# One-hot rows of a graph kernel's bucket pass: a single VectorE compare in place of GpSimd and ScalarE, and a transpose moved to the end of TensorE's step

## The reference

```python
# layers 1 and 2
z = concat([x[dst], x[src], attr]); m = sigmoid(z @ Wf + bf) * softplus(z @ Ws + bs)
h = leaky_relu(graph_norm(segment_sum(m, dst) + x))
x = layernorm(x + h)
# layer 3: row = src, col = dst
Wh = x @ W + b
sim = dot(Wh[row], Wh[col]) / max(|Wh[row]| * |Wh[col]|, 1e-8)
base = adj_v * softplus(deg_coeff[0] * deg_v + deg_coeff[1]) * (row != col)
pos = segment_sum((base * relu(sim))[:, None] * Wh[col], row)
neg = segment_sum((base * -relu(-sim))[:, None] * Wh[col], row)
out = layernorm(x + scale * (c0 * pos + c1 * neg + c2 * Wh))
```

## Time and profile before

| | |
|---|---|
| median of 3 runs | 10625.85 us |
| the profiled execution, its own time | 10622.02 us |
| its span, first to last instruction | 10620.5 us |
| instructions | 99188 |
| mean granted TensorE clock | 0.68 of full speed |
| busy: TensorE, weight loads | 6468.3 us (61%), 4406.6 us (41%) |
| busy: VectorE, ScalarE | 4393.9 us (41%), 3006.0 us (28%) |
| busy: GpSimd | 5852.2 us (55%) |

### The profile page before, as it was taken

How to read it: one execution, slowest core, us unless ns; L and a number is a source line. 1 busy time by engine, 2 the same in 40 slices (tenths; PEclk the granted TensorE clock), 3 DMA queues, 4 the chain that set the end, 5 groups by cost and what they waited for, 6 DMA issues and landing times.

```text
span 10620.5 us, 99188 instructions
## 1 busy us (share of the span) xinstructions
PE 6468.3 (61%) x22770; PEld 4406.6 (41%) x22771; DVE 4393.9 (41%) x7869; ACT 3006.0 (28%) x4649; POOL 5852.2 (55%) x5556
## 2 busy tenths in 40 slices
PE   0288888881477877771444444444666666666665
PEld 0144444441244444441322222224666666666665
DVE  3555555553344444444544444443222222222324
ACT  0144444441244444441222222222222222222221
POOL 6777777775777777775677777773111111111111
PEclk9988888885688888885566666665555555555555
DMA  8344444442233333331222222221000000000000
GB/s 306 101 129 130 132 128 132 128 132 95 79 102 103 101 103 103 103 97 27 60 63 63 63 63 63 63 62 30 21 21 20 21 21 21 20 22 20 21 20 22
DMA packets 561624, 798.10 MB, mean 75 GB/s; under 512 B 162586, under 2 KB 306858, under 8 KB 553354
## 3 DMA queue, kind: packets, MB, share of 16 engines
q1 hardware_dynamic: 371912, 482.15, 15.0%
q0 software_dynamic: 172640, 195.75, 8.7%
q10 hardware_dynamic: 16994, 119.45, 2.7%
HBM read 497.93 MB, written 298.87 MB: 75 GB/s over the span
## 4 chain that ended last, share of the span: by engine, by line
PE 20%; POOL 19%; issue 6%; ACT 5%; DVE 1%; DMA 0%; POOLq 0%; DVEq 0%; ACTq 0%; SPq 0%
POOL rows_by_src_bucket L693 14%; PE ps_two L859 8%; PE ps_gv L842 5%; POOL arena L718 4%; PE ps_out L868 4%; PE ps_pos L868 4%; ACT arena L1003 2%; ACT arena L1004 2%; DMA rows_by_src_bucket<-arena,put_idx 0%; POOLq L619 0%; DVE arena L1340 0%; DVE arena L1343 0%; DVE arena L1348 0%; ACT arena L980 0%; DVE H L1180 0%
## 5 line engine op out<-in xcount | busy, mean ns | idle before, releaser
L693 POOL DMA_INDIRECT rows_by_src_bucket<-arena,put_idx x1568 | 1606.2, 1024 | 494.0 <-issue 440.8
L625 POOL DMA_INDIRECT G<-h_rows,src_idx x1568 | 1532.6, 977 | 477.9 <-issue 477.9
L625 POOL DMA_INDIRECT G<-in_x,src_idx x1470 | 1546.7, 1052 | 448.0 <-issue 441.3
L842 PE MATMUL ps_gv<-ident,arena 128*128 128x128 f32 x1984 | 486.9, 427 | 1125.7 <-ACT arena L1004 1124.3
L754 PE MATMUL ps_gv<-arena,w_src 128*128 128x512 f32 x1568 | 1001.2, 774 | 0.0
L751 PE MATMUL ps_gv<-attr,w_attr 65*128 65x512 f32 x1568 | 983.8, 761 | 0.0
L816 PE MATMUL ps_pos<-arena 128*128 128x392 f32 x390 | 325.9, 939 | 1048.1 <-DVE arena L1193 1048.1
L859 PE MATMUL ps_two<-arena 128*128 x3968 | 872.7, 410 | 85.1 <-issue 85.1
L859 PEld LDWEIGHTS ps_two<-arena 128*128 128x128 f32 x3968 | 865.7, 330 | 109.5 <-issue 109.5
L842 PEld LDWEIGHTS ps_gv<-ident,arena 128*128 128x128 f32 x1984 | 388.6, 223 | 1172.1 <-ACT arena L1004 637.1
L1231 DVE TENSOR_SCALAR arena<-ps_gv 128x512 f32<-128x512 f32 x392 | 267.0, 681 | 1257.9 <-PE ps_gv L757 1257.5
(11 more groups left out here) (224 smaller groups left out, 11308.4 us busy)
## 6 DMA issues: line engine op xcount, KB each, us to landing
inj<-first_edge_rows SPq DMA_DIRECT2D x588, 256.0 KB, 3.2
running_sums<-arena SPq DMA_DIRECT2D x392, 256.0 KB, 2.4
same<-same_dst SPq DMA_DIRECT2D x1176, 64.0 KB
rows_by_src_bucket<-zeros ACTq DMA_DIRECT2D x62, 1072.0 KB
first_edge_rows<-zeros ACTq DMA_DIRECT2D x56, 896.0 KB, 5.6
attr<-in_attr_t SPq DMA_DIRECT2D x392, 128.0 KB, 3.5
G<-h_rows,src_idx POOLq DMA_INDIRECT x1568
rows_by_src_bucket<-arena,put_idx POOLq DMA_INDIRECT x1568
```

The lines of the kernel that those rows point to most:

```text
L625: pool.indirect_dma_start(out_, None, table_in, bass.IndirectOffsetOnAxis(ap=index, axis=0)).then_inc(s, 16)
L693: pool.indirect_dma_start(bucket_d, bass.IndirectOffsetOnAxis(ap=put_idx[:, buf, k:k + 1], axis=0), put[:, buf, k], None).then_inc(s_added ...
L842: mm = pe.transpose(turned_ps[:, buf % 2, k], onehot[:, buf % NB, k], ident[:])
```

## The change

In the bucket pass, GpSimd's `measure_rows` and ScalarE's `make_marks` are gone, with the semaphore between them. VectorE gets `mark_rows`, one compare (`is_equal`) of 128x1024 fp32 that writes `onehot` directly, with the same two waits as `measure_rows`; it stands third in VectorE's step, for the unit three ahead, and for units 0 to 2 ahead of the loop. In TensorE's step, `turn_marks` for the unit two ahead moves from first to last place. `mark_buckets` reads the fp32 tile `lane` in place of the bf16 `lane_b`, which is gone; `bucket` and `hot` stay bf16.

```diff
-            def measure_rows(h, buf):
-                wait(s_unit[buf], h * 16 + 16)
-                wait(s_outs, udone(h, buf, NB))
-                row_now = rows[buf].rearrange("p a (j f) -> p (a j) f", f=RW)[:, :, ROW_AT]
-                pool.tensor_tensor(onehot[:, buf % NB], across(lane[:], SLOTS), along(row_now, P),
-                                   ALU.subtract).then_inc(s_away, 1)
-
-            pipeline(pool, (measure_rows, 0), n=NU, trips=UTRIPS)
...
-            pipeline(pe, (turn_marks, -2), (pick, 0), (sum_unit, 1), n=NU, trips=UTRIPS)
+            pipeline(pe, (pick, 0), (sum_unit, 1), (turn_marks, -2), n=NU, trips=UTRIPS)
...
-            def make_marks(h, buf):
-                both = onehot[:, buf % NB].rearrange("p k e -> p (k e)")
-                act.wait_ge(s_away, udone(h, buf))
-                steps.then(nc.scalar.activation(both, both, ACT.Abs))
-                nc.scalar.activation(both, both, ACT.Relu, bias=1.0, scale=-1.0).then_inc(s_onehot, 1)
-
...
-            pipeline(act, (copy_marks, -1), (roots, 0), (make_marks, -3), steps=steps, per=NU, n=NU, trips=UTRIPS)
+            pipeline(act, (copy_marks, -1), (roots, 0), n=NU, trips=UTRIPS)
...
-                v.tensor_tensor(hot[:, buf % 2].rearrange("p (k t) -> p k t", t=NT), across(lane_b[:, 0:NT], SLOTS),
+                v.tensor_tensor(hot[:, buf % 2].rearrange("p (k t) -> p k t", t=NT), across(lane[:, 0:NT], SLOTS),
                                 along(bucket[:, at], NT), ALU.is_equal).then_inc(s_hot, 1)
...
+            def mark_rows(h, buf):
+                dve.wait_ge(s_unit[buf], h * 16 + 16)
+                dve.wait_ge(s_outs, udone(h, buf, NB))
+                row_now = rows[buf].rearrange("p a (j f) -> p (a j) f", f=RW)[:, :, ROW_AT]
+                v.tensor_tensor(onehot[:, buf % NB], across(lane[:], SLOTS), along(row_now, P),
+                                ALU.is_equal).then_inc(s_onehot, 1)
+
...
-            pipeline(dve, (weigh, 0), (add_unit, 2), steps=steps, per=8 * NU, n=NU, trips=UTRIPS)
+            for buf in range(3):
+                mark_rows(0, buf)
+            pipeline(dve, (weigh, 0), (add_unit, 2), (mark_rows, -3), steps=steps, per=8 * NU, n=NU, trips=UTRIPS)
```

More of the change, by code:

```diff
@@ L147, in gnn @@
         lane = sb("lane", [P, P])
-        lane_b = sb("lane_b", [P, P], BF16)
         half_i = sb("half_i", [P, TILES], I32)
@@ L350, in gnn @@
         s_unit = [sem(f"unit_loaded_{i}") for i in range(NU)]
-        s_away = sem("row_distances_ready")
         s_onehot = sem("row_onehot_ready")
@@ L365, in gnn @@
                   s_sumt, s_turned, s_sums, s_wt, s_hot, s_counted, *s_below, *s_ranked, *s_reached, s_pidx, s_sq, s_norm,
-                  s_put, s_away, s_onehot, s_att, s_atc, s_wr, s_n2, s_nn, s_dotted, s_wm, s_outs, s_hadd]
+                  s_put, s_onehot, s_att, s_atc, s_wr, s_n2, s_nn, s_dotted, s_wm, s_outs, s_hadd]
         by_sp = [s_ahead_st, s_table, s_out_st, s_stored]
@@ L1054, in _ @@
             then(v.tensor_copy(lane[:], lane_i))
-            then(v.tensor_copy(lane_b[:], lane_i))
             then(v.tensor_copy(half_id[:], half_i[:]))
```

## The result

The changed kernel takes 9021.17 us, the median of 4 runs (9016.43 to 9029.22), against 10624.85 us (10610.93 to 10627.47) for the kernel before in the same runs. The ratio is 0.8494, with a 95% interval of 0.8479 to 0.8508. The forecast was 9000 us.

What follows compares the result with a forecast made beforehand. The bucket pass was taken as bound by a ring of waits, 13.30 us a unit; opened, VectorE or TensorE decides by the clock: 7332.4 us plus 247 units at 6.75 us gives 9000 us, range 8830 to 9220.

Steps and rivals of the forecast that it cites:

- The ring, and that the turn's place closes it: Bucket pass: turn, first in TensorE's step, waits for rows needing the previous sum; 13.30 us a unit, opened by moving it.
- TensorE's own time, 8.48 us at 1.2 GHz: Bucket pass: turn, pick and sum together need 8.48 us a unit at 1.2 GHz, 4.24 at 2.4 GHz.
- The register loads should hide: TensorE, every fourth pick: loads that cost 0.34 us a unit would run while sum and turn still run.
- VectorE's own time, 6.08 us: Bucket pass, per unit: 4.64 for weigh and additions, 0.23 wait, 1.21 new compare; 5.84 to 6.78 us.
- The new waits: VectorE's `mark_rows` waits for the sum one unit back and should find it done, 3.41 us against at least 4.07.
- The standstill that I expected before the turn: At the high clock TensorE idles 1.84 us a unit in two parts, one before the turn, waiting for the compare.
- The fp32 bucket compare, 0: Placing and layer 1: the compare on fp32 costs the same 965 ns as on bf16, so 0 us.
- Start and end: First `weigh` about 5.5 us sooner, at 7262.5; 68.4 us from the last `weigh` to the end kept.
- Which engine: the mix: Bucket pass: TensorE's clock alternates, 0.6 up plus 0.05, giving 6.75 us a unit and 9000 us; chance 0.74.
- neither rival at one level: TensorE's clock stays up, 6.08 us a unit, 8834 us, chance 0.14; or down, 8.48, 9427 us, chance 0.10.
- the forecast's own formula: Bucket pass: units come at 0.65 / 6.08 + 0.35 / 8.48 a us; the time is 7332.4 + 247 times us a unit.
- The clock's rules: TensorE: a turn within unbroken work can raise the clock, against the skill's rule on transposes; sub-microsecond gaps may drop it.

Runs made afterwards that it cites:

- 1: The changed kernel with the turn first again in TensorE's step, one-hot rows still on VectorE: 10247.77 us, ratio 0.9647.
- 2: The kernel before with one edit, the turn last in TensorE's step, rows still made by GpSimd and ScalarE: 9228.44 us, ratio 0.8684.
- Experiment 6: The changed kernel with TensorE's register loads ahead of the sum and turn before every fourth pick: 9971.1 us, ratio 0.8563, on a chip where the kernel before takes 11648.6.
- experiment 5: The changed kernel with the bucket compare back on bf16 lane numbers: 10038.44 us, ratio 0.8612, on a chip where the kernel before takes 11648.64.
- experiment 8: The changed kernel with both TensorE's and VectorE's register loads early: 9846.68 us, ratio 0.8449, on a chip where the kernel before takes 11648.6.
- 7: The changed kernel with VectorE's register loads early, behind the compare's dispatch: 10040.69 us, ratio 0.8613, on a chip where the kernel before takes 11648.6.
- 9: The changed kernel with four idle 128x128 transposes added behind each pick on TensorE: 9106.29 us, ratio 0.857.
- 10: The changed kernel with both TensorE's and VectorE's register loads early and four idle transposes behind each pick: 8832.73 us, ratio 0.8312.
- 12: The changed kernel with ScalarE alone making the rows, turn last, both engines' register loads early and four idle transposes: 8888.11 us, ratio 0.8343.

## Why the prediction was right

*The ring, and that the turn's place closes it.* Right, and shown from both sides by 1 and 2: 11.76 us a unit with the turn first (I had reckoned 11.4 for it before the run), 7.62 with it last and the old engines.

*TensorE's own time, 8.48 us at 1.2 GHz.* Right. From the sum at 8064.24 to the next at 8072.67, both at the lower clock, it is 8.43 us.

*The register loads should hide.* Wrong. 77.2 us of issue in 205 units is 0.38 us a unit, no less than before. The turn behind which they stand waits itself for VectorE at the high clock, so the sequencer comes to them late. VectorE's compare on which the turn of 8032.66 depends, and the group of the turns, with no idle time ahead of it:

```profile
8030.83 1.23 DVE L1372 TENSOR_TENSOR arena<-lane,inj 128x1024 f32<-128x1024 f32 x1
...
L831 PE MATMUL ps_gv<-ident,arena 128*128 128x128 f32 x1640 | 303.2, 347 | 0.0
```

The compare ends at 8032.06. Until then the sequencer stands at the turn, the loads begin behind it, and the pick starts at 8036.05. Experiment 6 prices them at 0.35 us a unit, some 86 us of the profiled pass (67 by the medians).

*VectorE's own time, 6.08 us.* The compare was sized right, 1.226 us for 1.21. The 0.23 us ahead of it was too much: for most units the compare follows the additions at once. Where VectorE is the bound, units take 5.3 and 6.4 us by turns (without and with register loads), 5.8 in the mean.

*The new waits.* The compare finds the sum done: its only waits in the whole stretch, 6.4 us in 26 cases, are for the additions. What I overlooked is an old wait: the sum needs the additions of the unit two back, which stand behind `weigh` on VectorE. I had put the standstill before the sum down to `w_msg` alone; it is longer by the additions and their register loads, up to 1.79 us. The standstill that I expected before the turn does not show: TensorE is idle for 0.0 us ahead of L831, since the compare ends while the sum still runs. The second standstill is that of the register loads.

*The fp32 bucket compare, 0.* Right: 965 ns with either, and experiment 5 shows no difference. The Trainium skill ("VectorE: DVE Perf Modes", "What auto-detection actually checks") lets a tensor_tensor make two results a cycle if all its tensors are 16 bits wide and read with step 1. I took this to speak against the edit and put the missing gain down to the broadcast operands. The rule has that already: `bucket` repeats one element in the innermost dimension (`along`), which is step 0, so the compare is outside it, and the 965 ns agree. My own argument from the trace was weaker than it looked, since two durations always lie on one line; it is experiment 5 that shows it.

*Start and end.* From the last `weigh` to the end it is 9027.7 - 8959.3 = 68.4 us, to the tenth. The first `weigh` came 10.7 us behind the first load of the pass (7265.69 to 7276.39); before it was 19.6 (7248.48 to 7268.03). So 8.9 us sooner, where I reckoned 5.5. The pass itself began 17 us later than in the execution before; the placing loop is unchanged, and the first `weigh` of the profiled executions on such chips lies between 7267.4 and 7281.5 us, so that is the spread between executions, and it hides part of the gain in the profiled one.

*Which engine: the mix.* Right in kind: the clock goes up and down, and neither rival at one level came (8834 and 9427 us). It is up for (0.75 - 0.50) / 0.50 = about half of the time, not 0.6. VectorE's shorter time makes up for it: T is 6.81 for 6.75. In the forecast's own formula 0.5 alone would give 6.97 us a unit, 9053 us, and 5.8 us for VectorE alone 6.52, 8943 us; both together give 6.76. So the time is within 0.3% of the forecast by two errors that cancel, which is luck. VectorE is busy for 72% of the pass, where I had said over 80.

*The clock's rules.* The Trainium skill ("TensorE: Matmul & The Clock Gate", "PE-mode transpose") says that transposes don't count as work for the clock. Here all 55 rises stand in a pick right behind a whole turn, and none in a sum, which has a whole pick right ahead of it: that speaks against the page. It is no proof, for no kernel was run without the turn, and 28 of the 83 picks that have sum and turn at the lower clock right ahead of them bring no rise (none of the 55 in experiment 8). The same page ("Why this matters for your kernels") has the clock stay up but for long idle gaps between bursts; it fell behind 2.34, 1.79 and 1.89 us.

What is still open: what sets the share of time that the clock is up. It is 0.72 with TensorE busy for 92% (7), 0.86 with 90% (8), and idle transposes hardly move it (9, 10). That the standstills cause the falls is read from where they stand, not shown alone. And the falls are not the whole of it: between the changed kernel and 8 they are as frequent, and what differs is how soon the clock comes back, for which no run isolates a cause. A third and fourth PSUM place for the sums might take away the wait for the additions; it was not tried.

## What to carry to other kernels

When an engine waits in a ring, look first at the order of its own queue: moving one look-ahead step behind the work that it doesn't depend on gave 1396 of 1604 us, and changing the engine that feeds it 207 more. Once the ring is open, count for every engine all that stands between its pieces, register loads and the release of PSUM places among them, since the clock fell behind such standstills here. Two such edits should be tried together before one is dropped: VectorE's register loads were worth nothing alone and half a microsecond a unit beside TensorE's.

## What the runs showed of the hardware

- A 1.91 us tensor_tensor of GpSimd can hold up VectorE's small operations on SBUF: 1.90 us for one of 8 columns that takes 0.17 us otherwise (experiment 2, mean 605 ns over 183 of them).
- TensorE's clock can lock to a loop: in the changed kernel the same pattern returns every eight units, 54.62 us. Three picks with the long standstill, from TensorE's timeline:

```profile
7435.27 2.21 PE L848 MATMUL ps_two<-arena 128*128 x16 [2.34 <-issue]
...
7489.89 2.22 PE L848 MATMUL ps_two<-arena 128*128 x16 [2.34 <-issue]
...
7544.52 2.23 PE L848 MATMUL ps_two<-arena 128*128 x16 [2.34 <-issue]
```

- Four transposes more a unit did not hold TensorE's clock up: 0.76 for 0.75 (experiment 9), 0.89 for 0.86 (10), 0.81 for 0.83 (12). The falls became fewer and the low stretches longer.
- A register load costs much on a sequencer: 8 values for TensorE keep it from issuing until the pick starts 2.34 us late, 4 values keep VectorE idle for 1.03 to 1.17 us.
